# Probability strips and normalized tiles turned by DMA transposes in a one-layer attention and feed-forward kernel

## The reference

```python
x = L0_attn_x                                        # (1, 8192, 2048) f32
x = x + LN(attention(LN(x)))                         # 32 heads of 64
x = x + LN(ffn(LN(x)))                               # LN = layernorm, eps 1e-5

# attention: keys i-8 <= j < i+8 only
attn = (q @ k.T) * scale
attn = where(m != 0, attn * m, -inf)                 # m = (8 - |i-j|/2) / 8 in the window
out  = softmax(attn) @ v                             # then out @ proj_w.T + proj_b
# ffn: the input is normalized with ln_weight, ln_bias
out  = xn @ sign(weight).T * max|weight| * gamma + beta
```

## Time and profile before

| | us |
|---|---|
| median of 3 runs (676.54 to 702.75) | 677.22 |
| the profiled execution's own time | 676.98 |
| its span, slowest core (core 2) | 675.4 |
| spans of the eight cores | 670.2 to 675.4 |
| TensorE busy, of that span | 627.9 |

### The profile page before, as it was taken

The page is one execution under the profiler, slowest core; times in us unless marked ns, Lnnn a source line. Parts: engine busy times, 40 slices in busy tenths (PEclk is TensorE's granted clock), DMA queues, the critical chain, the costliest instruction groups (busy, mean ns, idle before and its releaser), DMA issues.

```text
span 675.4 us, 13044 instructions; the slowest of 8 cores (670.2 to 675.4 us)
## 1 busy us (share of the span) xinstructions
PE 627.9 (93%) x3736; PEld 339.1 (50%) x3792; DVE 419.4 (62%) x806; ACT 347.5 (51%) x1024; POOL 244.7 (36%) x394
## 2 busy tenths in 40 slices
PE   0799999999999999999999998898889999999992
PEld 0554444445666666666666665443444544444441
DVE  5885101114677777777777777425899867776565
ACT  3352010102778888888888888514345333342443
POOL 6112232113766666777766667400001000000000
PEclk9999999999999999999999999999799999999997
DMA  8999959911446656656666664985435567254553
GB/s 220 264 238 224 158 94 156 162 26 15 68 92 126 122 125 124 123 124 126 124 126 126 125 126 77 164 197 165 177 126 191 185 182 254 76 174 133 171 195 125
DMA packets 18390, 98.07 MB, mean 145 GB/s; under 512 B 2306, under 2 KB 2306, under 8 KB 12034
## 3 DMA queue, kind: packets, MB, share of 16 engines
q0 software_dynamic: 10944, 67.11, 45.4%
q1 hardware_dynamic: 7378, 30.12, 16.2%
HBM read 114.00 MB, written 16.78 MB: 194 GB/s over the span
## 4 chain that ended last, share of the span: by engine, by line
PE 79%; DMA 13%; DVE 3%; issue 3%; ACT 1%; POOL 1%; DVEq 0%; ACTq 0%; POOLq 0%; SPq 0%
PE bank L625 33%; PE bank L689 24%; PE bank L586 13%; DMA xbuf<-x_shard 5%; DMA Wp<-proj_wt 5%; DMA xre<-x_shard 3%; PE bank L641 2%; PE bank L649 2%; PE bank L662 2%; PE bank L786 1%; DMA fwstage<-ffn_wt 1%; DVE bnst L968 1%; PE bank L602 1%; PE bank L650 0%; DVE abuf L1195 0%
## 5 line engine op out<-in xcount | busy, mean ns | idle before, releaser
L625 PE MATMUL bank<-lnT,wbf 128*128 128x347 bf16 (+2 forms) x1249 | 244.5, 337 | 1.6
L625 PEld LDWEIGHTS bank<-lnT,wbf 128*128 128x128 bf16 x1280 | 122.9, 98 | 83.6
L894 ACT ACTIVATE tstrip<-tstrip,soft 128x144 f32<-128x144 f32 x256 | 103.0, 403 | 37.4 <-DVE soft L1088 36.5
L472 POOL TENSOR_TENSOR tstrip<-tstrip,maskb 128x288 f32<-128x288 f32 x128 | 93.4, 731 | 74.7 <-DVE tstrip L1011 74.5
L689 PE MATMUL bank<-Wp,attnT 128*128 128x512 bf16 x500 | 113.4, 382 | 2.3 <-DMA Wp<-proj_wt 0.7
L586 PE MATMUL bank<-vwbf,lnT 128*128 128x512 bf16 x499 | 111.5, 381 | 1.5 <-DMA vwbf<-v_w 0.6
L689 PE MATMUL bank<-Wf,attnT 128*128 128x512 fp8e4 x512 | 111.2, 379 | 0.0
L1011 DVE TENSOR_TENSOR tstrip<-bank,maskm 128x288 f32<-128x288 f32 x128 | 58.1, 454 | 49.6 <-PE bank L641 48.1
L689 PEld LDWEIGHTS bank<-Wp,attnT 128*128 128x128 bf16 x512 | 49.9, 99 | 60.2 <-issue 4.1
L689 PEld LDWEIGHTS bank<-Wf,attnT 128*128 128x128 bf16 x512 | 50.0, 98 | 59.7
L586 PEld LDWEIGHTS bank<-vwbf,lnT 128*128 128x128 bf16 x512 | 49.7, 98 | 60.1 <-issue 2.3
(11 more groups left out here) (113 smaller groups left out, 746.2 us busy)
## 6 DMA issues: line engine op xcount, KB each, us to landing
fwstage<-ffn_wt SPq DMA_DIRECT2D x32, 512.0 KB, 6.0
wbf<-qk_strips POOLq DMA_DIRECT2D x32, 512.0 KB, 6.9
xbuf<-x_shard POOLq DMA_DIRECT2D x8, 1024.0 KB, 17.5
Wp<-proj_wt POOLq DMA_DIRECT2D x4, 2048.0 KB, 33.8
xre<-x_shard POOLq DMA_DIRECT2D x8, 1024.0 KB, 8.4
y_scratch<-abuf POOLq DMA_DIRECT2D x8, 1024.0 KB, 5.7
ybuf<-y_scratch SPq DMA_DIRECT2D x8, 1024.0 KB, 7.5
out<-fbuf POOLq DMA_DIRECT2D x7, 1024.0 KB, 9.4
```

Source lines behind the costliest of these rows:

```text
L472: g_.tensor_add(ts3(g)[:, 2 * i:2 * i + 2, :], ts3(g)[:, 2 * i:2 * i + 2, :], window(maskb, g, i)).then_inc(biased, 1)
L625: last = t.matmul(qkbanks[gg % 3][:, 0:wd], wslot(2 * ph + is_k)[:, kc * 128:(kc + 1) * 128], lnT[:, kc * TOK + c0:kc * TOK + c0 + wd], st ...
L894: last = s.activation(ts3(m)[:, u, :], ts3(m)[:, u, :], AF.Exp, bias=neg_max(m)[:, u:u + 1], accum_out=total(m)[:, u:u + 1])
```

## The change

`LAG_T` goes from 3 + 3 to 3 + 4: the values of step g are computed one G later. `NBANK` goes from 6 to 8. TensorE's `transposes(g)` and the 128 transposes of the tail are gone, and so are the copies of their results from PSUM, except for the two small ones that build `ptail`. In their place SyncE issues one DMA transpose for each attention step, from the whole strip to `ptbuf` (now 640 columns a slot), and one for each tail tile, from `xnb` straight into `attnT`. The rotated identity `rolled` is not made any more. The loads of the weight strips 2 to 28 move from SyncE's to ScalarE's queue. The first six projection groups, not four, are filled in after the last qk group.

```diff
-LAG_T = LAG_S + 3
+LAG_T = LAG_S + 4
-NBANK = 6
+NBANK = 8
-    mbanks = [banks[7], banks[2], banks[0], banks[1], banks[3], banks[4]]
-    tpe = [banks[5][:].bitcast(BF16), banks[6][:].bitcast(BF16)]
+    mbanks = [banks[7], banks[2], banks[0], banks[1], banks[3], banks[4], banks[5], banks[6]]
-    early = [(i, kc) for i in range(4) for kc in range(14)]
+    early = [(i, kc) for i in range(6) for kc in range(14)]
@@ SyncE
-            for i in range(32):
-                if i >= 2:
-                    q.wait_ge(signed, i - 1)
-                    q.wait_ge(amaxed, i - 1)
+            for i in range(2):
                 q.dma_start(out=fw_slot(i), in_=fw_strip(i)).then_inc(fw_in[i % 2], 16)
+            for g in range(STEPS):
+                q.wait_ge(normed, g + 1)
+                if g >= 2:
+                    q.wait_ge(o_mm, g - 1)
+                q.dma_start_transpose(out=pt(g).rearrange("p (u c) -> p u c", c=128), in_=p_all(g)).then_inc(p_tr[g % 2], 16)
+            for i in range(ATT_STRIPS + 2, 32):
+                q.wait_ge(signed, i - 1)
+                q.wait_ge(amaxed, i - 1)
+                q.dma_start(out=fw_slot(i), in_=fw_strip(i)).then_inc(fw_in[i % 2], 16)
+            def turn(j):
+                q.wait_ge(xn_made, j + 1)
+                q.dma_start_transpose(out=attnT3[:, :, 128 * j:128 * j + 128], in_=xb(j)).then_inc(xn_tr[j], 16)
...
+            turn(0)
+            turn(1)
             q.wait_ge(all_max, 1)
             q.dma_start(out=sc_scr[None, :], in_=srow[:]).then_inc(max_out, 16)
...
+            for j in range(2, 6):
+                turn(j)
             q.wait_ge(bank_mm, gidx[("p", NT - 1, 3)] + 1)
             q.dma_start(out=gam[:], in_=bias_bc[1]).then_inc(gb_in[0], 16)
             q.dma_start(out=bet[:], in_=bias_bc[2]).then_inc(gb_in[1], 16)
+            load_y(0)
+            load_y(1)
+            turn(6)
+            turn(7)
@@ GpSimd, before the multiplication of step r_
                     if r_ >= 2:
-                        g_.wait_ge(p_tr, r_ - 1)
+                        g_.wait_ge(p_tr[r_ % 2], 16 * (r_ // 2))
@@ TensorE
-            def transposes(g):
-                t.wait_ge(normed, g + 1)
-                if g:
-                    t.wait_ge(p_ev, g)
-                for u in range(4):
-                    t.transpose(tbank[:, u * 128:u * 128 + 128], pu(g)[:, u, :], ident[:])
-                last = t.transpose(tbank[:, 512:640], p_ends(g), rolled[:])
-                last.then_inc(p_tr, 1)
...
                 if stage == "f":
-                    t.wait_ge(tev_v, t_ + 1)
-                    t.wait_ge(tev_s, t_ + 1)
+                    t.wait_ge(xn_tr[t_], 16)
...
-                        t.wait_ge(xn_made, j + 1)
-                        for half in range(2):
-                            if j:
-                                t.wait_ge(tev_v if half == 0 else tev_s, j)
-                            for k8 in range(8):
-                                kc = half * 8 + k8
-                                last = t.transpose(tpe[half][:, k8 * 128:(k8 + 1) * 128],
-                                                   xb(j)[:, kc * 128:(kc + 1) * 128], ident[:])
-                            last.then_inc(half_tr, 1)
@@ ScalarE
                 if step(h):
-                    s.wait_ge(p_tr, h + 1)
+                    s.wait_ge(p_tr[h % 2], 16 * (h // 2 + 1))
                     if h >= 2:
                         s.wait_ge(o_mm, h - 1)
-                    s.copy(pt(h), tbank[:, 0:512])
                     for i in range(2):
-                        last = s.copy(pt_end(h, i), tbank[64 * i:64 * i + 64, 512:528][:, None, :].broadcast_to([64, 2, 16]))
+                        last = s.copy(pt_end(h, i), pt(h)[64 * i:64 * i + 64, 624:640][:, None, :].broadcast_to([64, 2, 16]))
...
+                if att_strip(G - 1) is not None:
+                    i = att_strip(G - 1) + 2
+                    s.wait_ge(amaxed, i - 1)
+                    s.wait_ge(signed, i - 1)
+                    s.dma_start(out=fw_slot(i), in_=fw_strip(i)).then_inc(fw_in[i % 2], 16)
...
@@ VectorE, before it writes xb(c)
                     if c >= 2:
-                        v.wait_ge(half_tr, 2 * (c - 2) + 2)
+                        v.wait_ge(xn_tr[c - 2], 16)
```

More of the change, by code:

```diff
@@ L89, in build_program @@
     at_f = at_v + 16 * VROW * 2
-    size_f = 69760
+    size_f = 70272
     nc.alloc_sbuf_tensor("arena", [128, at_f + size_f - nc.sbuf_base], U8)
@@ L96, in build_program @@
     ident = place("identb", 128, BF16, at_small)
-    rolled = place("rolledb", 128, BF16, at_small + 256)
     tst = place("tst", NT * 16, F32, at_small + 512)
@@ L129, in build_program @@
     tstrip = place("tstrip", 12 * KWIN, F32, at_f + 55936)
[L130 to L133, removed]
+    ptbuf = place("ptbuf", 2 * PSTEP, BF16, at_f + 62848)
+    ptail = place("ptail", 2 * 64, BF16, at_f + 65408)
+    maskm = place("maskm", SW, BF16, at_f + 65664)
+    maskb = place("maskb", SW, BF16, at_f + 67968)
     lnw = place("lnw", D, BF16, at_f + 8192)
@@ L243, in build_program @@
     normed = sem("normed")
-    p_tr = sem("p_transposed")
+    p_tr = [sem("p_transposed0"), sem("p_transposed1")]
     p_ev = sem("p_evacuated")
@@ L276, in p_ends, with p_all @@
         return pstrip[:, (g % 2) * PSTEP + 512:(g % 2 + 1) * PSTEP]
+    def p_all(g):
+        return pstrip[:, (g % 2) * PSTEP:(g % 2 + 1) * PSTEP]
     def pt(g):
-        return ptbuf[:, (g % 2) * 512:(g % 2 + 1) * 512]
+        return ptbuf[:, (g % 2) * PSTEP:(g % 2 + 1) * PSTEP]
     def pt_end(g, i):
@@ L352, in build_program @@
     xn_made = sem("t_xn_made")
-    half_tr = sem("t_half_transposed")
-    tev_v = sem("t_tr_evac_v")
-    tev_s = sem("t_tr_evac_s")
+    xn_tr = [sem(f"t_xn_transposed{j}") for j in range(NT)]
     col_max = sem("t_col_max")
@@ L406, in job @@
         return 0 <= j < NT
-    def turned(s):
-        return s - 3 if job(s - 3) else None
     with nc.Block() as blk:
@@ L435, in _ @@
             q.dma_start(out=bet[:], in_=bias_bc[2]).then_inc(gb_in[1], 16)
[L436 to L440, removed]
+            load_y(0)
+            load_y(1)
+            turn(6)
+            turn(7)
+            for t_ in range(2, NT):
+                load_y(t_)
             for ng in range(4):
@@ L671, in tail_mm @@
                 for kc in range(k0, k1):
-                    if i < 4 and kc in (0, 14, 15):
+                    if i < 6 and kc in (0, 14, 15):
                         t.wait_ge(o_evv, 4 * max(kc + 1, 14))
@@ L684, in tail_mm @@
                             t.wait_ge(q_ev, 32)
-                        elif i >= 4:
+                        elif i == 7:
+                            t.wait_ge(o_evv, STEPS)
+                            t.wait_ge(o_evs, STEPS)
+                        elif i == 4 or i == 5:
                             t.wait_ge(masked, 2 * STEPS + i - 5)
@@ L737, in _ @@
                     v_tile(n, 0, 16)
-            t.wait_ge(padded, 4)
+            t.wait_ge(padded, 3)
             for G in range(STEPS + LAG_T):
@@ L747, in between @@
                         p = 4 * (G - STEPS) + part
-                        for i, kc in early[p * 56 // (4 * LAG_T):(p + 1) * 56 // (4 * LAG_T)]:
+                        for i, kc in early[p * 84 // (4 * LAG_T):(p + 1) * 84 // (4 * LAG_T)]:
                             tail_mm(i, kc, kc + 1)
-                if step(h):
-                    transposes(h)
                 between(0)
@@ L762, in _ @@
                     values(h)
-            for i in range(4):
+            for i in range(6):
                 tail_mm(i, 14, 16)
-            for i in range(4, len(lead)):
+            for i in range(6, len(lead)):
                 tail_mm(i, 0, 16)
@@ L777, in _ @@
                         tail_mm(gidx[(stage, t_, ng)], 0, 16)
-                    j = turned(s_)
-                    if ng == 0 and j is not None:
-                        t.wait_ge(xn_made, j + 1)
-                        for half in range(2):
-                            if j:
-                                t.wait_ge(tev_v if half == 0 else tev_s, j)
-                            for k8 in range(8):
-                                kc = half * 8 + k8
-                                last = t.transpose(tpe[half][:, k8 * 128:(k8 + 1) * 128],
-                                                   xb(j)[:, kc * 128:(kc + 1) * 128], ident[:])
-                            last.then_inc(half_tr, 1)
         @blk.scalar
@@ L946, in _ @@
                                      bias=fin[:, 13:14]).then_inc(last_centred, 1)
-                if turned(s_) is not None:
-                    s.wait_ge(half_tr, 2 * turned(s_) + 2)
-                    dst, src = halfT(turned(s_), 1)
-                    s.copy(dst, src).then_inc(tev_s, 1)
                 if job(j):
@@ L1069, in _ @@
                     v_copy(n)
-            v.wait_ge(padded, 4)
+            v.wait_ge(padded, 3)
             v.wait_ge(mask_in[0], 16)
@@ L1200, in _ @@
```

(4 more changed lines are left out.)

12 lines of the change are left out of this document (5 added, 7 removed).

## The result

| | before | changed |
|---|---|---|
| median, us | 689.99 (676.54 to 795.24, 4 runs) | 783.97 (778.29 to 789.93, 4 runs) |
| span of the profiled execution, slowest core | 675.4 (core 2) | 788.3 (core 5) |

The ratio of changed to before is 1.159, 95% interval 1.138 to 1.179: slower by 16%, about 107 us against the 677.2 of the kernel before. The forecast was 648 us, faster, with a range of 640 to 728.

A forecast was written before the change was run, and what follows sets the result against it. TensorE was taken to bound the kernel, busy 627.9 of 675.4 us. From 676.98 us, 16.2 for attention and 16.0 for the tail came off and 3 for the drain was added: -29.2, giving 648 us, range 640 to 728.

The forecast's parts named there:

- the landing time: Attention: L, a strip's transposing DMA landing, taken as 5 us, between 2.3 us from below and 11.5 from above.
- the attention term: Attention: five TensorE transposes a step gone, 0.28 us, for 58 steps up to the last qk group: 16.2 us saved.
- The price of the transposition itself: DMA engines, four attention steps: transposes add 0.66 MB, 3.3 us at the present price per byte.
- The DMA engines fill up: Rival, attention: engines full from 1.4 us a strip, q and k weights late; 664 us at twice, 771 at four times; chance 0.10.
- The ring sets the step: Rival, attention: landing of 7.6 us or more makes steps slower, blocks perhaps turned in series; 728 to 802 us; chance 0.16.
- The ring and its 6.6 us: Attention's softmax ring: step T at least (L + 1.2) / 2, TensorE's new step 3.9 us, so DMA hidden up to L = 6.6.
- The ring closes late but not fatally: Rival, attention: L of 6.6 to 8.0, T from 3.9 to 4.6, 648 to 690 us; chance 0.14.
- The drain: After the last qk group: seven more strips compete with the `Wp` load, 2 us lost, plus 1 us for the clock.
- The tail, 16.0 us: Tail: 7.1 us of transposes, 6.9 us of two waits and 2.0 us of lower clock saved.
- Eight banks: Tail's ring: eight banks cover VectorE's residual sums with 2.3 us margin; if this fails, 2 to 5 us once.
- ScalarE's 27 issues: Weight strips from ScalarE's queue: 9 us of issue against 38 us idle and 38 us of copies gone; costed at nothing.
- the order of `gam` and `bet`: Tail: they queue on SyncE behind tile 5's transposition; `bet` lands about 550, needed at 563, so even 10 us delay is hidden.

The follow-up runs named there:

- the DMAs by themselves: No kernel computation: strip transpositions or plain copies from SyncE, one after another, alone and beside various loads; a transposition landed in 2.7 us alone, 6.4 and 12.2 beside four converting loads.
- a ring of three: Changed kernel with three slots instead of two for pstrip, ptbuf and ptail, values one index later again, projection bias loaded after the last values: 727.0 us (one run).
- the two runs with and without `Wp`: Changed kernel without q and k loads of phases 2 to 15: 673.59 us; the same also without loading the last two quarters of `Wp`: 648.57 us.
- The plain-copy cases: DMAs only: the same 128 x 640 strip copied instead of transposed, alone and beside four converting loads: 2.1 us alone, 9.4 and 5.0 beside; in 256-byte pieces 2.5 and 14.1.

## Why the prediction was wrong

**The step that failed** is the landing time: "I take 5 us, since the weight strips' row is nearest in place and three times the size", and "That is under 6.6, so the attention term stands whole." The median was 5.8 in the profile after, but in every phase a transposition beside the converting q and k loads took 10 to 16 us in the chain, up to 17.8 at most, and one beside `Wp` 27.4. The row relied on, 6.0 us for 512 KB in the same window, showed that a large load gets its share beside another load. It did not show what becomes of a DMA made of some 670 packets of about 240 bytes (4032 for six in the DMAs by themselves), and the 2.3 us row showed an idle DMA system. In a ring the longest landing of each phase counts, not the median.

**The price of the transposition itself** was nearly right: "Transposes add 0.66 MB: 3.3 us at the same price", 0.8 us a strip, against 1.1 us in the kernel when alone (0.263 x 8 us / 1314 packets x 672) and 0.8 us in the DMAs by themselves. In attention the packets' times then grew: 0.61 x 228 = 139 us in the window of the earlier trace rows, 0.95 x 318 = 302 us for about the same steps now, and 0.49 x 213 = 104 us without the q and k loads. But these sums contain waiting. That the rival "The DMA engines fill up" had a price of 771 us at four times per byte, near the 784 measured, is a coincidence: a ring of three, with the same DMAs, went to 727 us and moved 138 GB/s. Of the rivals "The ring sets the step", 728 to 802 us at 0.16, had the mechanism, though not the cause: it let every landing be long, because the blocks are turned in series, where the runs show one stall in four steps, because of the loads beside it.

**Point by point.**
- Attention's term, 16.2 us: right in mechanism and size when the loads are away. Without them TensorE is 99% busy up to the last qk group, which ends at 399 us instead of 415.
- The ring and its 6.6 us: right in mechanism. TensorE waited behind L876 and GpSimd behind the DMA, as written, and a third slot took the waits from 95.4 to 5.8 us. The clock was not in the price: 0.84 in attention, and 21 us more for the projection matmuls. Waits of 119 us, less the 18 us of transposes saved, plus these 21 are 122 us, against the 120 between this kernel and the one with only the tail changed.
- The sum of the rival "The ring closes late but not fatally" is slightly off: at T = 3.9 it gives 645 us, not 648, since it counts 64 steps where the forecast counts 58.
- The drain, 2 us + 1 us: wrong by an order of magnitude. `Wp`'s two 2 MB loads hold one or two transpositions; 31.9 us in two waits without the q and k loads, and 25 us of time between the two runs with and without `Wp`.
- The tail, 16.0 us: 13 measured. TensorE's part went as forecast (16.5 us at the last matmul); the sum left out that VectorE and ScalarE end the run, 3 us later behind it. Eight banks are worth 3.4 us, within the 2 to 5 of the prediction.
- ScalarE's 27 issues and the order of `gam` and `bet` cost TensorE no wait.
- The Trainium skill's figure of 1309 ns for a 128 x 128 transposition by DMA (VectorE: DVE Perf Modes, "The three transpose paths") does not add up block by block: five blocks landed in 2.6 to 2.8 us here when alone.
- The 261 GB/s of the Trainium skill (DMA: Bandwidth & Descriptors, "Latency and other measured facts") would be 0.63 us a strip, by estimate. The page gives it for a middle dimension that is not contiguous, and the strip's is contiguous. The run of DMAs alone has about 0.8 us of all engines (29.9% of 16 us for six).

**What stays open.** Why packets of both queues get so long together in the kernel's stall (1119 ns for the load's), when the same loads and transpositions by themselves left the load's at 387 ns, was not settled. One difference is untested: in the kernel two transpositions were in flight at once (issued at 204.32 and 207.77 us, landed after 16.2 and 17.2), by themselves one at a time. What makes the 256-byte copy (14.1 us) worse than the 1280-byte one (9.4 us) is open too. The plain-copy cases show that transposing is not needed for it.

## What to carry to other kernels

A DMA inside a ring that other engines wait for must be priced beside the largest load that can be in flight with it, not by a median or by a row of big transfers: here 2.7 us became 6 beside one load, 12 beside four, 10 to 18 in the kernel's attention and 27 beside its 2 MB loads. Before moving work from a full engine to the DMA queues, mark in the trace when large loads run; where a step has many slots of slack (the tail's tiles) the move pays, where it has two (attention's strips) it needs to have no load beside it; a third slot took back 57 of the 120 us here. When TensorE's work in the last stage gets shorter, look at what the other engines still have to do after its last matmul: 3 of the 16 us were lost there.

## What the runs showed that was not expected

- A plain 164 KB copy from SBUF to SBUF went from 2.1 to 9.4 us beside four converting loads; in 256-byte pieces from 2.5 to 14.1 us.
- The last of four 512 KB loads landed after 15.0 us when converting f32 to bf16 on GpSimd's queue, after 7.2 us as bf16 there and 6.3 us as bf16 on ScalarE's (core 1). The conversion shows on every core read, the queue does not: on cores 3 and 5 the last two are 0.1 us apart.
- SyncE needed 1.19 us to issue a transposition of 640 columns, against 0.33 us for a 512 KB load; the one issued at 529.6 us, beside the load of `Wp`, held it for 14.7 us.
